# First attention: one product for the maxima ahead of the value products in each unit and one behind them

## The chip, the cores and the metric

The kernel runs on one core of one Trainium2 chip. The time is the device time of one execution in microseconds (us), and the figure compared is the median of several runs. The engines work side by side and meet at semaphores: TensorE (PE, its weight loads shown apart as PEld), VectorE (DVE), ScalarE (ACT), GpSimd (POOL) and the DMA queues, here above all SyncE's (SP).

## The reference

The whole is two layers over 8 images of 384 tokens and 256 channels: edges of an image joined with text, a first attention, an FP4 feed-forward, an anchor attention and a mixture of experts. The change touches the first attention alone:

```python
q, k, v, kp = (_heads(x @ W.T) for W in (W_Q, W_K, W_V, W_K_prime))   # 16 heads of 16
attn   = softmax(q k^T / 4)
attn_p = softmax(q kp^T / 4)
out = alpha * (attn v) + (1 - alpha) * (attn_p v)
return out @ W_O.T
```

16 heads times the two kinds of keys (k and kp) are 32 softmaxes over 384x384 scores for each image.

## The kernel before

`attention0` (from L122) writes out the instruction stream of each engine. `for_images` (L286) calls a function `turn` for images 0 to 7: images 1 to 4 in a hardware loop of two images a pass, the others straight. Text and trace are told here by these names.

**A unit** is one softmax: `turn` (L568 on PE) runs 32 units v for image i, in groups of four (g = v // 4, j = v % 4). In a unit PE issues, in this order:

- S: the transposed scores (`scores`, matmul at L516), two products into banks 4 and 5, then after one R a third into bank 6. ACT turns them into `prob` by exponentials (L706).
- R: products for the maxima (`ring`, L503). The softmax of the next image needs the maximum of each row of its scores, so the scores of image i+1 are computed a first time in the other orientation, 128x384 a product, and DVE reduces each to one maximum a row (`tensor_reduce`, L819). There are 96 such entries for an image, and two entries (48 and 97) that are a transpose of the maxima found (T, L500), from which DVE makes the negated maxima `mneg` (L823, L826) for SP to spread (L322). The entries use banks 0 to 2 in turn: entry r waits until the reduction of entry r-3 has ended (`ring_free`), and a T until all earlier ones have. The first entry of an image waits for all of the image before.
- V: the value products (`values`, L527), four heads side by side in 32 columns each, eight records in bank 7. They belong to the group before: V of units j = 1, 2, 3 is one third each. Units with j = 0 have none, nor have units 1 to 3 of image 0.
- a step in bank 3, where `BANK3` names one for the unit: projections of a later image (L473, L481), transposes (L464, L536, L542) or the output product (L550). It waits until the other engines have emptied bank 3 from the step before.

`ring_part(v)` gives a unit three entries, here called R1, R2 and R3; units 15 and 31 have a fourth, T. DVE's `turn` (L907) reduces the unit's entries and then does its part of the step: `low_parts` (L808), `normalize` (L841, L845), `add` (L854) with the moments behind it (L861). At the start of an image it first does `inputs` (L797). Image 7 has no entries to make, since no image follows.

The order in a unit is thus S S R1 S V R2 R3 (T) step, and S S R1 S R2 R3 step where there is no V.

Of the kernel before, what the change touches and what calls it, by code (L numbers as in the profile page):

```python
# [121 lines left out]
def attention0(nc, G, x, txt, scharr, wq, wk, wv, wkp, wo, alpha, wgate, wup, wdown, fp4_dram):  # L122
# [18 lines left out]
    def ring_part(v):  # L141

        return range(NR * v // UNITS, NR * (v + 1) // UNITS)
# [19 lines left out]
    def edge_piece(r):  # L163

        j, n = divmod(r - len(PREPARE), len(TAPS))
        return (j + BESIDE, n) if 0 <= j < B - BESIDE else (None, None)
# [6 lines left out]
    def bank3(v, prev, more, more2):  # L173

        step, n = BANK3.get(v, (None, 0))
        of = {"turn_outputs": -1 if n >= GROUPS - 2 else 0, "values": 1, "turn_y": -1, "output": -1,
              "inputs": 2, "project": 2, None: None}[step]
        if step is None or not {-1: prev, 0: True, 1: more, 2: more2}[of]:
            return None, 0, 0
        return step, n, of  # L180

    with ExitStack() as ctx:
# [113 lines left out]
        with nc.Block() as block:  # L296
# [163 lines left out]
            def _(pe):  # L460
# [24 lines left out]
                def ring(i, b, entries):  # L485

                    for r in entries:
                        u, t = RING[r]
                        if r in (0, NR // 2):
                            for m in range(3):  # L490
                                signal = stack_in[r // (NR // 2)][m]
                                pe.wait_ge(signal.sem, signal.at(i, 16 * len(SLOTS)))

                        back = 3 if t is not None else 1
                        if r >= back:
                            pe.wait_ge(ring_free.sem, ring_free.at(i, r - back + 1))
                        elif not isinstance(i, int) or i:
                            pe.wait_ge(ring_free.sem, ring_free.at(i, 0))
                        if t is None:
                            mm = pe.transpose(ps[0:2 * NM, r % 3, 0:P], mx[:, u:u + 2].rearrange("p n k h t -> p (n k h t)"),  # L500
                                              ident[:])
                        else:
                            mm = pe.matmul(ps[:, r % 3, 0:T], qs[0:NS, b, u // 2, t * P:(t + 1) * P],  # L503
                                           ks[0:NS, b, u % 2, u // 2], start=True, stop=True)
                        mm.then_inc(ring_full.sem, 1)

                def scores(i, b, v, part):

                    hh, kp = v // (2 * QUAD) * QUAD + v % QUAD, v // QUAD % 2
                    if v % HALF == 0 and part == 0:  # L510
                        signal = mrow_in[v // HALF]
                        pe.wait_ge(signal.sem, signal.at(i, signal.per))

                    pe.wait_ge(exp_done.sem, exp_done.at(i, max(2 * v + part - 1, 0)))
                    for t in PARTS[part]:
                        mm = pe.matmul(ps[:, 4 + t, 0:T], ks[0:NS + 4, b, kp, hh, t * P:(t + 1) * P],  # L516
                                       qs[0:NS + 4, b, hh], start=True, stop=True)
                    mm.then_inc(st_done.sem, 1)

                def values(i, b, g, t):  # L520

                    if t == 0:
                        pe.wait_ge(exp_done.sem, exp_done.at(i, 2 * QUAD * (g + 1)))

                        pe.wait_ge(o_done.sem, o_done.at(i, g))
                    for j in range(QUAD):
                        mm = pe.matmul(ps[j * SLOT:(j + 1) * SLOT, 7, 0:T],  # L527
                                       vp[:, b, t, g // 2 * QUAD + j], prob[:, g % 2, j, t],
                                       start=(t == 0), stop=(t == TT - 1), tile_position=(0, j * SLOT))
                    if t == TT - 1:  # L530
                        mm.then_inc(av_done.sem, 1)
# [27 lines left out]
                def in_bank3(step, i, n, last):  # L559

                    if last:
                        signal, image, count = last
                        pe.wait_ge(signal.sem, signal.at(image, count))
                    do, signal = STEPS[step]
                    do(i, n)
                    return signal, i, n + 1

                def turn(i, b, prev, more, more2):  # L568

                    last = (y_done, i - 1, GROUPS - 2) if prev else (rest_done, 1, 3 * KC)  # L570
                    for v in range(UNITS):
                        g, j = v // QUAD, v % QUAD
                        scores(i, b, v, 0)
                        if more:
                            ring(i + 1, 1 - b, ring_part(v)[:1])
                        scores(i, b, v, 1)
                        if j and g:
                            values(i, b, g - 1, j - 1)
                        elif j and prev:
                            values(i - 1, 1 - b, GROUPS - 1, j - 1)  # L580
                        if more:
                            ring(i + 1, 1 - b, ring_part(v)[1:])
                        step, n, of = bank3(v, prev, more, more2)
                        if step:
                            last = in_bank3(step, i + of, n, last)
# [55 lines left out]
                for r in range(FIRST):  # L641
# [3 lines left out]
                    i, n = edge_piece(r)  # L645
# [4 lines left out]
                pe.wait_ge(vp_ready.sem, 1)  # L650
                pe.wait_ge(mag_done.sem, mag_done.at(B - 1, 2))
                for_images(pe, turn)

                i = B - 1
# [1611 lines left out]
```

## Time and profile before

| | us |
|---|---|
| median of three runs | 1908.77 (1907.85 to 1909.83) |
| profiled execution, its own time | 1910.5 |
| span of the profile, first to last instruction | 1908.7 |
| of it, first attention's units with entries (images 0 to 6) | 140 to 666 |
| PE busy | 1774.1 (93%) |
| DVE busy | 1025.9 (54%) |
| ACT busy | 679.3 (36%) |
| DVE reductions for the maxima, L819, 768 of them | 383.6 |
| PE products R, L503, 768 of them | 221.6 |
| mean granted clock of PE | 0.974 of 2.4 GHz |

A row of the timeline has the start, the time from there to the end of the last of its instructions, the engine, the line, output and input, the count, and in brackets how long the engine had been idle and who released it. A single product's duration includes the way through the array, so products that follow each other closely start nearer together than they take. "x2" is two instructions merged into one row.

### The profile page before, as it was taken

Reading aid. Unit: us, or ns where it says so; the run is one execution under the profiler, and the core shown is the slowest. Engines: PE = TensorE matmul, PEld = TensorE weight load, DVE = VectorE, ACT = ScalarE, POOL = GpSimd, SP = SyncE. Lnnn points to the kernel's source line nnn. Section 1 sums busy time; section 2 is a strip of 40 time slices with the busy share of each in tenths; the row PEclk is TensorE's granted clock in tenths of the full one; section 3 lists DMA queues with packets and bytes.
Section 4 is the critical chain, followed back from the end, with each engine's and each line's share of the span. In section 5 each row is a group of like instructions: output and inputs, shape, how many; then the busy total and the mean of one; then the engine's idle time right before and its main releaser. Section 6 shows DMA issues by size and latency. Waiting matters only on the chain. (4 is left out here: it accounts for less than half of the span.)

```text
span 1908.7 us, 29136 instructions
## 1 busy us (share of the span) xinstructions
PE 1774.1 (93%) x9935; PEld 1121.4 (59%) x9935; DVE 1025.9 (54%) x2071; ACT 679.3 (36%) x1292; POOL 398.9 (21%) x415
## 2 busy tenths in 40 slices
PE   7989999899999994888899999997999999999997
PEld 3324444444444333566665656565666668999997
DVE  6587877777778874788876445542321121222221
ACT  2115656556556673444444223322211110111110
POOL 2101021020210001677662211220032121010010
PEclk9979999999999996999999999998999999999999
DMA  5833643635436023000009000000010012242211
GB/s 186 137 51 64 88 76 39 103 62 65 76 61 91 2 71 126 19 0 0 0 6 375 3 0 0 0 1 1 0 42 33 17 36 97 101 167 99 100 36 32
DMA packets 112675, 117.56 MB, mean 62 GB/s; under 512 B 11535, under 2 KB 104513, under 8 KB 112322
## 3 DMA queue, kind: packets, MB, share of 16 engines
q1 hardware_dynamic: 99330, 87.93, 21.8%
q10 hardware_dynamic: 9600, 18.92, 2.8%
q0 software_dynamic: 3648, 9.46, 1.3%
q8 instruction: 55, 0.90, 0.2%
q14 instruction: 42, 0.34, 0.1%
HBM read 80.87 MB, written 35.29 MB: 61 GB/s over the span
## 5 line engine op out<-in xcount | busy, mean ns | idle before, releaser
L819 DVE TENSOR_REDUCE mx<-ps_a 128x1 f32<-128x384 f32 x768 | 383.6, 551 | 70.0 <-PE ps_a L503 67.8
L706 ACT ACTIVATE prob<-ps_a 128x768 f32<-128x768 f32 (+1 forms) x512 | 306.2, 650 | 119.8 <-PE ps_a L516 119.7
L503 PE MATMUL ps_a<-ks,qs 96*128 96x384 bf16 x768 | 221.6, 340 | 12.0 <-DVE mx L819 4.7
L516 PE MATMUL ps_a<-qs,ks 100*128 100x384 bf16 x768 | 210.3, 334 | 6.5 <-issue 3.8
L2029 PEld LDWEIGHTS ps_e<-xTr,w 128*128 128x128 f32 x1792 | 204.4, 192 | 2.2 <-issue 0.8
L2029 PE MATMUL ps_e<-xTr,w 128*128 128x128 f32 x1792 | 204.7, 275 | 0.6 <-DVE xTr L2202 0.6
L1965 PE MATMUL ps_e<-xT_all,w 128*128 (+1 forms) x512 | 170.4, 492 | 0.9 <-ACT xT_all L2056 0.9
L503 PEld LDWEIGHTS ps_a<-ks,qs 96*128 96x128 bf16 x768 | 61.9, 98 | 181.0 <-DVE mx L819 119.9
L527 PE MATMUL ps_a<-prob,vp 128*32 128x384 f32 x1536 | 164.7, 502 | 0.0
L1514 PE MATMUL ps_m<-w 128*128 128x352 f32 x384 | 125.0, 470 | 21.7 <-ACT w L1677 21.3
L1965 PEld LDWEIGHTS ps_e<-xT_all,w 128*128 128x128 f32 x512 | 97.7, 192 | 66.5 <-issue 1.8
L2092 ACT ACTIVATE gel_r<-ps_e 128x512 f32<-128x512 f32 x56 | 33.5, 597 | 280.5 <-PE ps_e L2029 280.5
L516 PEld LDWEIGHTS ps_a<-qs,ks 100*128 100x128 bf16 x768 | 72.0, 99 | 75.8 <-ACT prob L706 27.2
L2109 DVE TENSOR_TENSOR hid_e<-gel,ps_e 128x384 f32<-128x384 f32 x64 | 35.5, 554 | 137.1 <-ACT gel L2062 137.1
L1514 PEld LDWEIGHTS ps_m<-w 128*128 128x128 f32 x384 | 70.3, 192 | 61.8 <-issue 23.9
L2062 ACT ACTIVATE gel<-ps_e 128x384 f32<-128x384 f32 x64 | 31.5, 492 | 207.9 <-PE ps_e L1965 207.9
L2038 PE MATMUL ps_e<-w,hid_r 128*128 128x256 f32 x448 | 101.3, 379 | 0.0
L1476 POOL TENSOR_TENSOR attn<-lg,gsum 128x1024 f32<-128x1024 f32 x24 | 45.6, 1901 | 234.9 <-DVE gsum L1378 234.9
L2213 DVE TENSOR_TENSOR hid_r<-gel_r,ps_e 128x512 f32<-128x512 f32 x56 | 38.5, 688 | 100.6 <-ACT gel_r L2092 100.6
L1581 PE MATMUL ps_m<-wsT,xT_a 128*128 128x512 f32 x192 | 87.1, 596 | 4.8 <-DVE lg L1369 4.8
L442 POOL TENSOR_TENSOR y<-y 128x192 f32<-128x192 f32 x32 | 19.9, 621 | 332.5 <-DVE y L845 332.5
L2038 PEld LDWEIGHTS ps_e<-w,hid_r 128*128 128x128 f32 x448 | 82.9, 190 | 10.1
(242 smaller groups left out, 2519.7 us busy)
## 6 DMA issues: line engine op xcount, KB each, us to landing
ks<-parts_dram SPq DMA_DIRECT2D x192, 96.0 KB, 6.3
w<-in_L_ffn_W_dram ACTq DMA_DIRECT2D x18, 1024.0 KB, 8.2
parts_dram<-parts SPq DMA_DIRECT2D x24, 576.0 KB, 3.9
qs<-parts_dram SPq DMA_DIRECT2D x96, 96.0 KB, 4.2
prob<-in_x_dram SPq DMA_DIRECT2D x24, 256.0 KB, 3.6
w<-in_L_ffn_W_dram SPq DMA_DIRECT2D x6, 1024.0 KB, 13.0
grouped_x<-empty_row SPq DMA_DIRECT2D x1, 4352.0 KB, 24.6
grouped_h<-empty_row SPq DMA_DIRECT2D x1, 4240.5 KB, 33.1
```

The lines of the kernel that those rows point to most:

```text
L503: mm = pe.matmul(ps[:, r % 3, 0:T], qs[0:NS, b, u // 2, t * P:(t + 1) * P], ks[0:NS, b, u % 2, u // 2], start=True, stop=True)
L516: mm = pe.matmul(ps[:, 4 + t, 0:T], ks[0:NS + 4, b, kp, hh, t * P:(t + 1) * P], qs[0:NS + 4, b, hh], start=True, stop=True)
L527: mm = pe.matmul(ps[j * SLOT:(j + 1) * SLOT, 7, 0:T], vp[:, b, t, g // 2 * QUAD + j], prob[:, g % 2, j, t], start=(t == 0), stop=(t == TT ...
L706: act.activation(prob[:, g % 2, j, ts.start:ts.stop], ps[:, 4 + ts.start:4 + ts.stop, 0:T], ACT.Exp).then_inc(exp_done.sem, 1)
L819: dve.tensor_reduce(at, ps[:, r % 3, 0:T], AX.X, ALU.max).then_inc(ring_free.sem, 1)
L1476: pool.tensor_tensor(attn[:, b, t].rearrange("p (h a) -> p h a", a=A1), lg[:, t % 2].rearrange("p (h a) -> p h a", a=A1), gsum[:, t % 2, 1 ...
L1514: mm = pe.matmul(ps[:, 2 * (u % 2) + n, 0:HALF0], xT[:, t, k], wguT[:, n, k, s * HALF0:(s + 1) * HALF0], start=(k == 0), stop=(k == KC - 1))
L1581: mm = pe.matmul(ps[:, bank + n], xT1[:, k, t * P:(t + 1) * P], wsT[:, k, n * 512:(n + 1) * 512], start=(k == 0), stop=(k == KC - 1))
L1965: mm = pe.matmul(ps[:, 2 * (a % 2) + m, 0:T], w12[:, 0, m, k, a * P:(a + 1) * P], xT_all[:, i, k], start=(k == 0), stop=(k == KC - 1))
L2029: mm = pe.matmul(ps[:, 2 * n + m, a * P:(a + 1) * P], w12[:, b, m, k, n * HALF1 + a * P:n * HALF1 + (a + 1) * P], xTr[:, k], start=(k == 0 ...
L2038: mm = pe.matmul(ps[:, 4, 0:C], hid_r[:, a], w3[:, b, a], start=(a == 0), stop=(a == IT1 - 1))
L2213: dve.tensor_tensor(hid_r[:, n * 4:(n + 1) * 4].rearrange("p a t -> p (a t)"), gel_r[:, n], ps[:, 2 * n + 1], ALU.mult).then_inc(rhid_done ...
```

## The change

In a unit, the second of its entries (R2) is issued ahead of V, straight behind the third score product, and the rest (R3, and T where there is one) stays behind V. Before, both stood behind V. The entries keep their numbers, banks and order among each other, and the number of instructions is the same. DVE, ACT, POOL and SP keep their order.

```diff
                         scores(i, b, v, 1)
+                        if more:
+                            ring(i + 1, 1 - b, ring_part(v)[1:2])
                         if j and g:
                             values(i, b, g - 1, j - 1)
                         elif j and prev:
                             values(i - 1, 1 - b, GROUPS - 1, j - 1)
                         if more:
-                            ring(i + 1, 1 - b, ring_part(v)[1:])
+                            ring(i + 1, 1 - b, ring_part(v)[2:])
```

Where a unit has no V the two calls follow each other and the order is the one before. With V it becomes S S R1 S R2 V R3 (T) step.

## Rows read from the trace of the kernel before

**Rows 1.** Stages view, image 1's stretch: busy time and count by engine, clock, DMA.

```profile
225.00:310.00 85.00, 80.95 (x533) 37.35 (x532) 65.44 (x144) 52.62 (x97) 11.43 (x17) 1.00 0.50 74
```

**Rows 2.** Waits of PE from 140 to 667: total, times, longest.

```profile
PE ps_a L500 <- DVE mx L819: 14.2, 15, 1.0
```

**Rows 3.** Instructions of tile ps_a: durations in ns (least, median, most), starts, forms.

```profile
L527 PE MATMUL ps_a<-prob,vp x1536: 486/498/849, 153.3 to 721.4; 128*32 128x384 f32 x192
...
L819 DVE TENSOR_REDUCE mx<-ps_a x768: 524/549/560, 76.7 to 665.7; 128x1 f32<-128x384 f32 x192
```

**Rows 4.** Timeline of unit 30 of image 1, without a step.

```profile
285.69 0.49 PE L516 MATMUL ps_a<-qs,ks 100*128 100x384 bf16 x2
...
286.18 0.33 PE L516 MATMUL ps_a<-qs,ks 100*128 100x384 bf16 x1
...
286.44 0.85 PE L527 MATMUL ps_a<-prob,vp 128*32 128x384 f32 x8
287.22 0.11 PEld L503 LDWEIGHTS ps_a<-ks,qs 96*128 96x128 bf16 x2 [0.62 <-DVE mx L819]
287.22 0.50 PE L503 MATMUL ps_a<-ks,qs 96*128 96x384 bf16 x2
...
287.56 0.49 PE L516 MATMUL ps_a<-qs,ks 100*128 100x384 bf16 x2
287.60 1.49 DVE L819 TENSOR_REDUCE mx<-ps_a 128x1 f32<-128x384 f32 x3 [0.38 <-PE ps_a L503]
```

**Rows 5.** Timeline: R2 and R3 of units without V, first, one in full, last.

```profile
159.73 0.80 PE L503 MATMUL ps_a<-ks,qs 96*128 96x384 bf16 x2
...
282.24 2.42 DVE L819 TENSOR_REDUCE mx<-ps_a 128x1 f32<-128x384 f32 x5 [0.38 <-PE ps_a L503]
...
282.86 0.79 PE L503 MATMUL ps_a<-ks,qs 96*128 96x384 bf16 x2
...
283.49 0.49 PE L536 MATMUL ps_a<-ident,osb 128*128 128x128 f32 x3
...
658.59 0.79 PE L503 MATMUL ps_a<-ks,qs 96*128 96x384 bf16 x2
```

**Rows 6.** Timeline: last reductions ahead of T in unit 31 of image 1.

```profile
289.47 1.02 DVE L819 TENSOR_REDUCE mx<-ps_a 128x1 f32<-128x384 f32 x2 [0.38 <-PE ps_a L503]
...
290.55 0.31 PE L500 MATMUL ps_a<-ident,mx 128*96 128x128 f32 x1 [0.95 <-DVE mx L819]
```

**Rows 7.** Timeline: the same in unit 15, behind a low_parts.

```profile
251.66 0.55 DVE L819 TENSOR_REDUCE mx<-ps_a 128x1 f32<-128x384 f32 x1
...
252.37 1.02 DVE L819 TENSOR_REDUCE mx<-ps_a 128x1 f32<-128x384 f32 x2 [0.16 <-PE ps_a L503]
...
253.45 0.31 PE L500 MATMUL ps_a<-ident,mx 128*96 128x128 f32 x1 [0.95 <-DVE mx L819]
```

**Rows 8.** Timeline of units 22 to 24 of image 1, behind the moments.

```profile
272.82 1.93 DVE L819 TENSOR_REDUCE mx<-ps_a 128x1 f32<-128x384 f32 x4
...
273.42 0.34 PE L503 MATMUL ps_a<-ks,qs 96*128 96x384 bf16 x1
...
275.63 0.80 PE L503 MATMUL ps_a<-ks,qs 96*128 96x384 bf16 x2
```

**Rows 9.** Timeline of units 0 to 2 of image 2, behind `inputs`.

```profile
292.98 1.48 DVE L819 TENSOR_REDUCE mx<-ps_a 128x1 f32<-128x384 f32 x3
...
293.59 0.34 PE L503 MATMUL ps_a<-ks,qs 96*128 96x384 bf16 x1 [0.49 <-DVE mx L819]
...
295.58 0.34 PE L503 MATMUL ps_a<-ks,qs 96*128 96x384 bf16 x1
```

**Rows 10.** Timeline of PE, image 7: first f32 products straight behind V.

```profile
697.28 0.92 PE L550 MATMUL ps_a<-wT,yT 128*128 128x256 f32 x3
```

**Rows 11.** Stages view: first units of images 1 and 2, columns as in Rows 1.

```profile
213.00:219.00 6.00, 5.29 (x25) 2.37 (x26) 4.43 (x12) 2.50 (x4) 0.00 (x0) 0.72 0.05 10
290.00:296.00 6.00, 4.58 (x28) 1.94 (x28) 5.01 (x15) 2.92 (x5) 0.00 (x0) 1.00 0.04 11
```

## The prediction

> **What bounds the kernel now.** I read the stages first, then the waits of PE, then the timeline of one image unit by unit. In the stretch of image 1 PE is busy 80.95 of 85 us at full clock, DVE 65.44, ACT 52.62 [rows 1]: PE sets the pace, and DVE, which only has to give three banks back in time, is the engine that makes it wait. The change moves work on PE from one place to another and takes nothing away. It can gain only what PE stands still for DVE, so those standstills have to be found and priced one by one. The waits view names one kind, the transpose T behind the last reductions: 14.2 us in 15 places [rows 2]. It hides the rest, because a product's recorded duration covers short holes; these have to be read from the distance of starts.
>
> A clean unit with V and without a step takes 287.56 - 285.69 = 1.87 us [rows 4]. Where products follow each other, starts are 0.165 us apart (two take 0.49 to 0.50, one 0.33). From the third S to V is 286.44 - 286.18 = 0.26, so 0.09 goes on the turn to the four narrow tiles. From V to R2 is 0.78, and R2 to the next S is 0.34, two products [rows 4]. DVE starts 0.38 after R2 does (287.60 against 287.22), and a chain of reductions takes 0.55 for the first and about 0.47 for each more (three in 1.49) [rows 4], although one alone takes 0.549 [rows 3]. From the end of a reduction to the product that waited for it is about 0.06.
>
> **The change part by part.** Unit with nothing late: S to R2 0.165, R2 to V 0.26, V to R3 0.78, R3 to the next S 0.165. That is the same 1.87. R2 has the shape of the S ahead of it, so I take 0.26 for the turn to the tiles as it stands, and the number of turns doesn't change. Effect 0, for 165 units (21 of image 0, 24 in each of images 1 to 6). The V records themselves are untouched (498 ns median) [rows 3]. V ends 0.165 later, and with it ACT's copy of bank 7; ACT has slack for that in the units where the copy stands, and the turn of its result comes a unit later.
>
> (a) Units without V. In these R3 comes only 0.99 us after the R3 of the unit before, and must wait for that one's reduction. In unit 28 of image 1 the two R records take 0.79 where 0.49 is the clean value: 0.30 us of standstill [rows 5]. The reason is that R2 and R3 of unit 27 come out together behind V, at 281.86 and 282.03. DVE starts at 282.24, needs 0.55 + 0.47 for the two, and is through at 283.26; R3 of unit 28 starts at 283.32. After the change R2 of unit 27 has been reduced while V ran, and R3 alone is behind V, at the same 282.03: reduction from 282.41 to 282.96, product free at 283.02, where its clean place is. I take 0.28 of gain (bounds 0.2 and 0.30, the whole standstill). Such records of 0.79 or 0.80 stand, the first at 159.73 and the last at 658.59 [rows 5], in units 8, 20, 24, 28 of image 0, units 24 and 28 of images 1 to 5, and units 12, 24, 28 of image 6: 17. Unit 24 of images 1 to 6 is special, next paragraph, so 11 x 0.28 = 3.1 us.
>
> (b) Unit 24 of images 1 to 6. Here DVE is behind by the moments. Its reductions of unit 22 start at 272.82 and end at 273.37, 273.83 and 274.30; R1 of unit 23 is held by the first until 273.42 [rows 8]. R2 of unit 23, moved ahead, would like to start 0.33 later at 273.75, but waits for the second, until 273.90: a new wait of 0.15, and V, R3 and all the rest stand behind it on PE. In return R3 of unit 24 (275.63, 0.80 for two [rows 8]) no longer waits. Net 0.30 - 0.15 = 0.15, six times: 0.9 us.
>
> (c) The transposes T. R2, R3 and T now: DVE starts at 289.47, takes 1.02 for two, T starts at 290.55, 1.46 after R2 [rows 6]. Changed: R3 starts 0.165 later than R2 did, its reduction 0.38 on, 0.55 long, T 0.06 on: 1.16. Gain 0.29. It holds for units 31 of images 0 to 6 and unit 15 of image 6, 8 places. In unit 15 of images 0 to 5 DVE begins R1's reduction late, at 251.66, behind a `low_parts` [rows 7]. Then R1 ends at 252.21, R2 at 252.68, R3 at 253.15, and T comes at 253.21 against 253.45 now: 0.24. Sum 8 x 0.29 + 6 x 0.24 = 3.8 us. What follows T (the negated maxima, `inputs`, the next image's R1) hangs on T and moves with it. Bounds: 0.2 and 0.47 (one reduction less with nothing given back) a place, so 2.8 to 6.6.
>
> To this last one the Trainium skill has a rule, in "VectorE: DVE Perf Modes", section "The DRAIN you can't avoid": a next operation doesn't start before the pipe of the one before has emptied. By it the pair would cost 2 x 0.549 and (c) would give some 0.08 more at each T, in all about 1 us. The rows of pairs say 1.02, so the trace disagrees, and I stay with the rows.
>
> (d) Places where the new R2 has to wait ahead of V. Rule: R2 of a unit waits for the second reduction of the unit before. It bites where DVE is late. In units 0 to 2 of image 2 the reductions of unit 0 start at 292.98 behind `inputs`, and R1 of unit 1 already waits for the first, until 293.59 [rows 9]. The second ends at 294.00, so R2 goes at 294.07 where it would like 293.92: 0.15. In unit 2 R1 waits until 295.58 now [rows 9], 0.11 late; changed, that wait is hidden in the delay, but R2 waits again, 0.12. Net loss 0.15 for images 2 and 4, where unit 1 has this standstill: 0.3 us. Images 1, 3 and 5 start at half clock and have no such wait, image 6 has no `inputs`. Behind `normalize` (units 26 and 30) I find R2 about 0.1 free. If that is misjudged it costs up to 0.1 in 14 units, 1.4 us. Behind `low_parts` the second reduction of the unit before is done long before.
>
> **The sum.** 3.1 + 0.9 + 3.8 - 0.3 = 7.5 us. All of it is on PE's path: PE runs the stage, the next stage starts behind a barrier, and image 7 is unchanged. SP's transfers for later images hang on DVE's and POOL's steps, which keep their places. The profiled execution took 1910.5 of its own, 1.8 over its span and 1.7 over the median; it would come to 1903.0, and the median of 1908.8 to 1901.3. With the bounds of (a), (c) and (d) the gain is 4.6 (2.2 + 0.9 + 2.8, less 0.3 and about 1) to 10.5 (3.3 + 0.9 + 6.6, less 0.3).
>
> **The rivals.**
>
> Half the gain. The places of (a) don't open, because the third bank is short again: R3's reduction ends 0.02 or less ahead of where R3 wants to go, so any delay of DVE by a tenth brings it back. Against it: in unit 28 DVE has been idle 0.38 before the R3 reduction [rows 5]. Only (c) is left, with 0.3 off: 3.5, the time 1905.3.
>
> Nothing. The standstills move from R3 and T to R2, as far as DVE is the real limit of those stretches, or something else is next late (ACT's exponentials, the emptying of bank 3). For it: around T several engines wait. Against it: DVE is idle before the reductions in question [rows 5, 6], so it isn't the limit. 1908.8.
>
> Slower: the load of weights isn't hidden behind a single product. Now two products of one shape stand between V and the rest, and their two loads are done together, 0.11 for both [rows 4]. Behind the change the load for a step's f32 product, or for S, has only one product of 0.165 to hide under. That loads can stick out behind V is seen where f32 products follow it directly: the first three take 0.92 [rows 10], 0.11 more than three starts 0.215 apart and a last duration of 0.38. If each of the 165 units paid about 0.10, that would be 16.5 us, less 7.5: 9.0 slower, 1917.8. It decides from 7.5 / 165 = 0.045 us a unit on. Against it: the second load starts at once in today's order, and R3's stream of 0.165 is longer than the 0.11. The Trainium skill speaks for this rival, in "TensorE: Matmul & The Clock Gate", section "Part 3: Packing small matmuls — row/col tiling": a load overlaps running matmuls only where the row groups differ, and these products use the same rows. The trace disagrees for plain products, whose loads start with the product before them.
>
> More: the clock. At half clock the first units of image 1 cost more than those of image 2: PE is busy 5.29 of 6 us for 25 products at a granted clock of 0.72, against 4.58 for 28 at 1.00 [rows 11]. The clock fell there behind T and the longer stop at the edge of the loop. Each of four such edges could be spared or moved by shorter stops: up to 0.8 us each, 2 us or so in all, 1899.3.
>
> **How the numbers follow.** Forecast 1901.3, chance 0.62. More by the clock 0.10, half 0.13, nothing 0.07, slower 0.08. A measurement of this kernel can tell about 0.2% from no change, 3.8 us; the line is at 1905.0. Half the gain falls on either side of it: 0.07 faster, 0.06 the same. Faster 0.79, same 0.13, slower 0.08. The forecast's own bounds give 1898.3 to 1904.2. With the half case taken in at one end and the clock at the other, 1898.8 to 1905.2 leaves out the cases of no gain and of slower (0.15) and a thin tail at the fast end, together under 0.2.
>
> **What would show it.** In unit 30, S to R2 0.165, R2 to V 0.26, V to R3 0.78 and 1.87 in all: if the unit is longer, the slower rival is at work. The two R of unit 28 back to 0.49. T's wait behind R3 about 0.99 after R3's start instead of 1.28. R2 of unit 23 and of unit 1 waiting about 0.15 ahead of V. The stretch from image 1's to image 2's T about 1 us shorter, and the first attention's last R 7.5 us earlier. DVE's busy time and its 768 reductions should stay. The prediction is wrong if ACT or the emptying of bank 3 shows up as the new releaser in these places, or if a wait ahead of V turns up in the units with steps.

## The result and the profile after

The changed kernel takes 1896.5 us, the median of 9 runs (1894.5 to 1898.8). The kernel before has a median of 1906.8 over nine runs, three of which are those that the prediction started from; one of the others took 6035.7 and is left out of the ratio. The ratio is 0.995, with a 95% interval of 0.9936 to 0.9964. That is a gain of 9.5 us (6.9 to 12.2) by the ratio, 10.3 between the medians, and 12.3 on the base of 1908.8 that the prediction was made against. The prediction said 1901.3 (1898.8 to 1905.2) and a gain of 7.5. The sign was right, and the time fell below the range.

The profiled execution took 1897.8, with a span of 1896.0, 12.7 less than before. Of the 12.7, 8.9 lie between the first S of image 0 and that of image 7 (517.4 against 526.3), where the change is; 0.1 lies ahead of it and 3.7 behind, in stages that the change doesn't touch. The head of the page of the changed kernel (busy time, share of the span, instructions):

```profile
PE 1768.3 (93%) x9935; PEld 1120.0 (59%) x9935; DVE 1022.3 (54%) x2071; ACT 682.5 (36%) x1292; POOL 398.9 (21%) x415
PEclk8989999999999997999999999998999999999999
```

The granted clock by slices on the page of the kernel before:

```profile
PEclk9979999999999996999999999998999999999999
```

The counts are the same and DVE's work is nearly so (1025.9 before); the time went out of holes on PE. The clock rows differ in three of the 40 slices: the first and the third (9 and 7 before, 8 and 8 here), both ahead of the units, and the sixteenth (6 before, 7 here), behind them. A slice is 47 us long, and a short stretch at half clock at the edge of an image doesn't show in it.

The stages view of the changed kernel, one stretch in image 1 (it answers to [rows 1]) and its edge (to [rows 11]). The image begins 1.9 us earlier here, and the windows are 5 and 3 us earlier, so they don't cut it at quite the same place:

```profile
220.00:305.00 85.00, 81.76 (x536) 38.51 (x536) 64.37 (x144) 52.53 (x96) 11.43 (x17) 1.00 0.52 79
210.00:216.00 6.00, 4.47 (x32) 1.64 (x24) 4.53 (x13) 3.49 (x7) 0.00 (x0) 1.00 0.02 3
```

PE gets 536 products into 85 us instead of 533, all at full clock. From the first S of image 1 to that of image 2 it is 75.46 instead of 76.96. From image 1's T to image 2's it is 75.57 instead of 76.25, both without an edge at half clock: 0.7 less, where the prediction had said about 1. At the edge of image 1, where before had a clock of 0.72, this execution has 1.00.

The waits of PE between 139 and 658 us, changed kernel (total, times, longest), against [rows 2]:

```profile
PE ps_a L500 <- DVE mx L821: 10.2, 15, 0.9
PE ps_a L503 <- DVE mx L821: 1.8, 4, 0.6
```

T waits 4.0 us less in its 15 places, of which 14 are in the units that changed (the first stands ahead of image 0). The predicted gain of 3.8 there is met.

**The places one by one**, from the timelines. First unit 28 of image 1, where R2 and R3 took 0.79 before [rows 5], and the start of unit 29 (rows: start, time to the end of the last, engine, line, output and input, count, in brackets idle time and releaser):

```profile
279.17 0.34 PE L503 MATMUL ps_a<-ks,qs 96*128 96x384 bf16 x1
279.35 0.49 PE L516 MATMUL ps_a<-qs,ks 100*128 100x384 bf16 x2
279.55 1.51 DVE L821 TENSOR_REDUCE mx<-ps_a 128x1 f32<-128x384 f32 x3 [0.36 <-PE ps_a L503]
279.87 1.19 ACT L708 ACTIVATE prob<-ps_a 128x768 f32<-128x768 f32 x2
280.00 0.49 PE L503 MATMUL ps_a<-ks,qs 96*128 96x384 bf16 x2
280.33 0.49 PE L536 MATMUL ps_a<-ident,osb 128*128 128x128 f32 x3
...
280.74 0.34 PE L516 MATMUL ps_a<-qs,ks 100*128 100x384 bf16 x1
```

The pair R2, R3 is back to 0.49, as forecast. But the unit, S to S, is 1.39 (280.74 - 279.35), and not the 1.32 that its products would need (six starts of 0.165 and three transposes in 0.33). The next S is now held by ACT, as the distances show: the exponentials start 0.52 after S, two take 1.19 together, the first about 0.81 of it, and the next S starts 0.06 after that, at 1.39. The trace of the kernel before has this length already where no R was late, as in unit 20 of image 5 (578.15 - 576.75, with the two R in 0.49):

```profile
576.75 0.49 PE L516 MATMUL ps_a<-qs,ks 100*128 100x384 bf16 x2
577.28 1.19 ACT L706 ACTIVATE prob<-ps_a 128x768 f32<-128x768 f32 x2 [1.98 <-PE ps_a L516]
577.41 0.49 PE L503 MATMUL ps_a<-ks,qs 96*128 96x384 bf16 x2
...
578.15 0.50 PE L516 MATMUL ps_a<-qs,ks 100*128 100x384 bf16 x2
```

Unit 31 of image 1, then T of unit 15:

```profile
284.98 0.33 PE L516 MATMUL ps_a<-qs,ks 100*128 100x384 bf16 x1
285.15 0.33 PE L503 MATMUL ps_a<-ks,qs 96*128 96x384 bf16 x1
285.40 0.85 PE L527 MATMUL ps_a<-prob,vp 128*32 128x384 f32 x8
286.19 0.34 PE L503 MATMUL ps_a<-ks,qs 96*128 96x384 bf16 x1
286.56 0.56 DVE L821 TENSOR_REDUCE mx<-ps_a 128x1 f32<-128x384 f32 x1 [0.36 <-PE ps_a L503]
287.18 0.31 PE L500 MATMUL ps_a<-ident,mx 128*96 128x128 f32 x1 [0.65 <-DVE mx L821]
```

```profile
250.66 0.31 PE L500 MATMUL ps_a<-ident,mx 128*96 128x128 f32 x1 [0.69 <-DVE mx L821]
```

The pattern of a unit is the predicted one: S to R2 0.17, R2 to V 0.25, V to R3 0.79, R3 to T 0.99. In front of T stands one reduction of 0.56, where [rows 6] had two in 1.02.

Unit 1 of image 2, with the new wait ahead of V. R1 is held as before [rows 9], and R2 comes 0.47 behind it, where 0.33 would be clean:

```profile
290.22 0.34 PE L503 MATMUL ps_a<-ks,qs 96*128 96x384 bf16 x1 [0.49 <-DVE mx L821]
...
290.69 0.34 PE L503 MATMUL ps_a<-ks,qs 96*128 96x384 bf16 x1
290.95 0.85 PE L527 MATMUL ps_a<-prob,vp 128*32 128x384 f32 x8
```

### The profile page after: what moved, and what is told of

Read it like the earlier page. It is cut to its first block and busy times, and to the rows that moved or that the text cites. A ratio compares the mean times of both kernels' runs of the same rounds, so it can differ in the third digit from the quotient of the medians.

```text
span 1896.0 us, 29136 instructions
## 1 busy us (share of the span) xinstructions
PE 1768.3 (93%) x9935; PEld 1120.0 (59%) x9935; DVE 1022.3 (54%) x2071; ACT 682.5 (36%) x1292; POOL 398.9 (21%) x415
## 5 line engine op out<-in xcount | busy, mean ns | idle before, releaser
L503 PE MATMUL ps_a<-ks,qs 96*128 96x384 bf16 x768 | 244.1, 338 | 10.0 <-DVE mx L821 5.5
L503 PEld LDWEIGHTS ps_a<-ks,qs 96*128 96x128 bf16 x768 | 74.5, 98 | 188.7 <-DVE mx L821 103.2
```

## The experiments

Each kernel's time was taken in five rounds against the kernel before on the same chip. Chips and rounds differ by more than some of the effects, so a ratio is always to the kernel before beside it. "Unit" lengths are the distance from S to the next S, in stretches at full clock, as differences from the kernel before. The diffs are in PE's `turn`, against the kernel before unless told otherwise.

**c_before and c_after**: the two kernels again, unchanged, as the measure for the rest.

> The kernel before, unchanged, measured again beside the others, for its spread and its granted clock. The profile of the changed kernel shows the forecast holes closing (about 6.6 us by their own sizes), yet the profiled span fell by 12.7. Theory A: the rest is the clock; the kernel before loses full clock at the edges of image 1, 3, 5 and 7, where PE stands still longest, and in most executions it shows a lower mean clock than the changed kernel: ratio 1.000, mean clock about 0.974, the changed one 0.979. Rival B: the difference of clocks is chance of the executions first shown; then both kernels have the same mean clock over ten executions, this one's median lies at about 1904, and the changed one is 6 to 7 us below it.

> The changed kernel, unchanged, on the same chip. Theory A (holes 6.6 us plus a higher clock): ratio about 0.995, mean granted clock higher by 0.003 to 0.005 than the kernel before in most executions. Rival B (chance of the clock): ratio about 0.9965, equal clocks.

Measured: the kernel before 1904.7 (12 runs, 1901.1 to 1907.5), after 1895.6 (6 runs), ratio 0.9955 (0.9941 to 0.997). The kernel before has a median of 1904.8 over 29 runs of this chip, 1906.1 over 23 on a second, 1904.5 over 12 on a third; single runs go from 1899.8 to 1912.0. The three runs that the prediction started from, with 1908.8, lie near the upper end of this. The mean clock is 0.9766 and 0.9793. So neither expectation holds whole: the kernel before isn't as slow as A had it, and the changed kernel's clock isn't the same, as B had it.

Comparing these two, unit by unit, gives what each place of the change is worth:

```
unit                                  measured   forecast
8, 20, 24, 28 of image 0; 12, 28 ...   -0.227     -0.28     (a), 11 places
23 of images 1 to 6                    +0.137     +0.15     (b)
24 of images 1 to 6                    -0.227     -0.30     (b)
31 of images 0 to 6, S to T            -0.30      -0.29     (c)
15 of images 0 to 5                    -0.257     -0.24     (c)
15 of image 6                          -0.30      -0.29     (c)
1 of images 1, 2 and 4                 +0.138     +0.15, images 2 and 4 only (d)
18 of image 6                          +0.083      0
the unit behind one that got shorter   +0.012      0
other units with V                     +0.003      0
```

Images 3 and 5 can't be compared at unit 1 in this pair, since the kernel before ran there at half clock. For image 5 the profile of e_fill, with the old order at full clock, has 2.26 and the changed kernel 2.40: +0.14 there too. Image 3 runs at half clock there in all twelve profiles.

**e_t_only**: R2 goes ahead in units 15 and 31 alone. **e_rest_only**: in all units but these.

```diff
+                        ahead = 2 if v in (15, 31) else 1      # e_t_only
+                        ahead = 1 if v in (15, 31) else 2      # e_rest_only
+                        if more:
+                            ring(i + 1, 1 - b, ring_part(v)[1:ahead])
...
-                            ring(i + 1, 1 - b, ring_part(v)[1:])
+                            ring(i + 1, 1 - b, ring_part(v)[ahead:])
```

> R2 goes ahead of V in units 15 and 31 alone, the other units keep the order of before. Forecast's part (c): 8 x 0.29 + 6 x 0.24 = 3.8 us, T 0.99 us after R3 (1.03 in unit 15 behind low_parts) instead of 1.28, and R3 of units 24 and 28 still held (the two R records 0.79). If the clock gain of theory A comes from shorter stops at T, this kernel has it too: gain 6 to 8 us and a mean clock like the changed kernel's. If the clock has to do with something else, the gain is 3.8.

> R2 goes ahead of V in all units but 15 and 31. Forecast's parts (a), (b) and (d): holes 3.1 + 0.9 - 0.3, by the sizes seen in the changed kernel's profile 3.2 + 1.0 - 0.6 - about 0.8 for units that became 0.005 us longer: 2.8 us. T 1.28 us after R3 as before. If shorter stops at T bring the clock gain, this kernel hasn't got it: gain about 3 us, mean clock like before. If the clock is chance, it lies anywhere between the two.

Measured: e_t_only 1900.8, ratio 0.9981 (0.9971 to 0.9992); e_rest_only 1903.8, ratio 0.9995 (0.9982 to 1.0009). In e_t_only the pair of unit 28 keeps its 0.80, and T waits 0.65 instead of 0.95:

```profile
276.16 0.80 PE L503 MATMUL ps_a<-ks,qs 96*128 96x384 bf16 x2
...
283.56 0.31 PE L500 MATMUL ps_a<-ident,mx 128*96 128x128 f32 x1 [0.65 <-DVE mx L822]
```

In e_rest_only it is the other way round:

```profile
284.78 0.50 PE L503 MATMUL ps_a<-ks,qs 96*128 96x384 bf16 x2
...
286.24 0.31 PE L500 MATMUL ps_a<-ident,mx 128*96 128x128 f32 x1 [0.95 <-DVE mx L822]
```

So the terms stand apart as the prediction had them, and no place pays for another: from unit 16 to 31 an image gains 0.28 by the one and 0.30 by the other, and 0.57 by both. The gain at the T's is larger than all the rest of the change together. The times are less additive than the units: against the runs of c_before, spans fall by 4.2 and 0.7 on average, and by 8.7 with both. The interval of e_rest_only includes no change, so its forecast gain of 2.8 stands in its units alone. What is missing goes with the clock, below. e_t_only also answers its own question: it has the shorter stops at every T and a mean clock of 0.9772, and not the 0.979 of the changed kernel.

**e_both_ahead**: R2 and R3 both ahead of V, so that nothing but V stands in front of the step.

```diff
+                        ahead = 3
```

> R2 and R3 both ahead of V in every unit. Against the changed kernel, by holes: T of unit 31 and of image 6's unit 15 comes about 0.46 us earlier (8 times, 3.7), unit 15 of images 0 to 5 is held by DVE behind low_parts and gains nothing, R3 gets its own wait ahead of V in units 1 and 2 of images 1 to 5 and in unit 23 of images 1 to 6 (about 0.3 each more, 2.5 and 1.8). Sum about 0.6 slower than the changed kernel: ratio 0.996. If clean units get longer by it, the turn to the tiles costs more than taken.

Measured: 1911.4, ratio 1.0021 (1.0011 to 1.0032), slower than the kernel before, although unit 31 is 0.745 shorter. The expectation, 0.6 slower than the changed kernel, was wrong: the units take 12.4 more than in c_after. The T's give 3.4, and the waits ahead of V in units 1, 2 and 23 cost 3.8, much as expected (unit 1 is now +0.43 and unit 23 +0.437 against before). What it lacked is 11.2 us. R3 also waits ahead of V in units 13, 17 and 21 and, behind `normalize`, in 26 and 30 (6.5 together, the dearer step of the first three included). And a step that stands directly behind V costs more in the others (4.7): units with projections or the output product +0.09, with transposes +0.04, although nobody is late there. The timeline of e_both_ahead at a projection:

```profile
256.65 0.62 PE L503 MATMUL ps_a<-ks,qs 96*128 96x384 bf16 x2
256.93 0.10 PEld L503 LDWEIGHTS ps_a<-ks,qs 96*128 96x128 bf16 x1 [0.34 <-DVE mx L822]
257.20 0.85 PE L527 MATMUL ps_a<-prob,vp 128*32 128x384 f32 x8
257.98 1.56 PE L473 MATMUL ps_a<-xT,wT 128*128 128x384 f32 x4
```

The four f32 products take 1.56; with one R product between V and them they take 1.46 (the next kernel's first row). The weight loads of these four products begin only at 257.98, together with the first of them, and the second product starts 0.43 behind the first, where the later ones start 0.32 apart. In the changed kernel the first of these loads begins under R3. This is the mechanism of the slower rival, at about the 0.11 that it read from [rows 10]. It needs V directly in front. One product of 0.165 in between hides the load fully: in the changed kernel nearly all units with steps are unchanged within 0.005.

**e_best**: what the places teach, put together. In unit 31 (and 15 of image 6) R2 and R3 go ahead of V, since there T has nothing else to wait for; in unit 15 of images 0 to 5 T goes behind the projection, which fills its wait; units 1 and 2 keep the old order; all others have the order of the change.

```diff
+                        late_t = v == 15 and more2
+                        ahead = 1 if v in (1, 2) else 3 if v == 31 or v == 15 and not more2 else 2
...
-                            ring(i + 1, 1 - b, ring_part(v)[1:])
+                            ring(i + 1, 1 - b, ring_part(v)[ahead:3 if late_t else None])
                         step, n, of = bank3(v, prev, more, more2)
                         if step:
                             last = in_bank3(step, i + of, n, last)
+                        if more and late_t:
+                            ring(i + 1, 1 - b, ring_part(v)[3:])
```

> The changed kernel, but: in unit 31 (and unit 15 of image 6) R2 and R3 both ahead of V; in unit 15 of images 0 to 5 T goes behind the unit's projection, which then fills the wait; units 1 and 2 keep the order of before. By holes, against the changed kernel: 8 x 0.46 = 3.7, 6 x about 0.5 = 3.2 (the wait of 0.8 filled, 0.1 given back at R3 of unit 16 and 0.2 at its low_parts), 0.14 in image 1 to 5 = 0.6. Together 7.5 us: about 1888, ratio 0.991 to 0.992. If the clock follows the stops, a little less time still. If the chain from T to the negated maxima is what sets the pace behind it, part of the 7.5 comes back as a wait of the next image's R1.

Measured: 1890.0 (1887.1 to 1892.4), ratio 0.9914 (0.9897 to 0.993), the fastest of all kernels here. Unit 31 is 0.75 shorter than before, unit 15 is 1.19 shorter (3.27), unit 16 is 0.38 longer, as the transposes there now wait for `rest`; unit 1 is back. Over the images the units take 7.2 us less than in c_after, near the 7.5 expected. Its timeline around T of unit 15 and of unit 31:

```profile
245.51 1.46 PE L473 MATMUL ps_a<-xT,wT 128*128 128x384 f32 x4
246.80 0.27 PE L500 MATMUL ps_a<-ident,mx 128*96 128x128 f32 x1
...
248.71 0.54 PE L536 MATMUL ps_a<-ident,osb 128*128 128x128 f32 x3 [0.54 <-DVE rest L814]
...
281.89 0.31 PE L500 MATMUL ps_a<-ident,mx 128*96 128x128 f32 x1 [0.30 <-DVE mx L825]
```

T waits for nothing in unit 15 and 0.30 in unit 31, where the changed kernel has 0.69 and 0.65.

**e_fill and e_after_fill**: the question of the clock. In unit 31 the stop ahead of T is filled with products that nobody reads (five in the kernel before, four in the changed kernel), and T's time isn't meant to move.

```diff
-                            ring(i + 1, 1 - b, ring_part(v)[1:])
+                            ring(i + 1, 1 - b, ring_part(v)[1:3])    # [2:] and [2:3] in e_after_fill
+                            if v == UNITS - 1:
+                                signal, image, count = last
+                                pe.wait_ge(signal.sem, signal.at(image, count))
+                                for _ in range(5):           # 4 in e_after_fill
+                                    pe.matmul(ps[:, 3, 0:T], qs[0:NS, 1 - b, H0 - 1, 0:P],
+                                              ks[0:NS, 1 - b, 1, H0 - 1], start=True, stop=True)
+                            ring(i + 1, 1 - b, ring_part(v)[3:])
```

> The kernel before, with five more products of R's shape into bank 3 (whose content nobody reads any more) in the standstill ahead of T of unit 31 of images 0 to 6. They run 5 x 0.165 = 0.83 us inside a wait of about 1.28, so T comes when it came and the holes theory alone says: no change, ratio 1.000. They leave PE standing 0.45 us there instead of 1.28. Theory A (shorter stops at an image's edge keep the clock up): mean granted clock over the executions rises from 0.9765 towards 0.979 and the time falls by 2 to 4 us. Rival B (the clock has to do with something else, the stops' length doesn't matter): clock 0.9765, ratio 1.000.

> The changed kernel with four such products ahead of T of unit 31 (0.66 us inside a wait of about 0.99). Theory A: clock 0.979 or a little more, time as the changed kernel or 1 us below it, ratio 0.9955 to 0.995. Rival B: the same time as the changed kernel.

The timeline of e_fill shows that T stays where it was, 1.45 behind R2, with PE at work until then:

```profile
287.97 0.50 PE L503 MATMUL ps_a<-ks,qs 96*128 96x384 bf16 x2
288.31 0.98 PE L587 MATMUL ps_a<-ks,qs 96*128 96x384 bf16 x5
289.42 0.31 PE L500 MATMUL ps_a<-ident,mx 128*96 128x128 f32 x1
```

Measured: e_fill 1904.7, ratio 0.9993 (0.9982 to 1.0005), mean clock over its runs 0.9771 against 0.9757 of the kernel before beside it; e_after_fill 1897.6, ratio 0.9951 (0.9935 to 0.9967), clock 0.9792. In the kernel before the clock rises a little, in the changed kernel (0.979 in its first runs) it doesn't. That fits shorter stops as a part of the reason, but the interval of e_fill includes no change, and its clock goes half of the way at most: a hint, not shown.

**e_long**: the changed kernel with an extra reduction, whose result nobody reads, ahead of the last one before T in unit 31, so that T is late again while everything else has the new order. **c_after2**: the changed kernel, unchanged, beside it.

```diff
+        spare = sb("spare", [P, 1])
...
+                            if r == NR - 2:
+                                dve.tensor_reduce(spare[:], ps[:, r % 3, 0:T], AX.X, ALU.max)
                             dve.tensor_reduce(at, ps[:, r % 3, 0:T], AX.X, ALU.max).then_inc(ring_free.sem, 1)
```

> The changed kernel with one reduction more on DVE, made a first time into a spare tile and not used, ahead of the last reduction of unit 31 of images 0 to 6. PE's stop at T there grows by about 0.5 us, to 1.5 behind R3 in place of 0.99, longer than in the kernel before; everything else stays. By holes alone: 7 x 0.5 = 3.5 us more than the changed kernel, clock as the changed kernel's (0.979). Theory A (the length of the stops at an image's edge decides how often the clock falls): mean clock down to about 0.9765 and 5 to 7 us more. Rival B: 3.5 and the clock stays at 0.979.

> The changed kernel once more, for its mean clock and as the neighbour of the next one. As before it: ratio 0.995 to 0.9955, mean granted clock about 0.979 against 0.9757 to 0.9765 of the kernel before.

Measured: c_after2 1898.7, ratio 0.9969 (0.9958 to 0.9981), a gain of 5.8 at nearly equal clocks (0.9776 against 0.9769); the 0.979 and the ratio of 0.995 that were expected didn't come again. e_long 1917.0, ratio 1.0069. Its unit 31 is 0.47 longer than that of the changed kernel, as forecast:

```profile
284.72 0.56 DVE L823 TENSOR_REDUCE spare<-ps_a 128x1 f32<-128x384 f32 x1 [0.36 <-PE ps_a L504]
285.20 0.55 DVE L824 TENSOR_REDUCE mx<-ps_a 128x1 f32<-128x384 f32 x1
285.80 0.32 PE L501 MATMUL ps_a<-ident,mx 128*96 128x128 f32 x1 [1.12 <-DVE mx L824]
```

From the T ahead of image 0's first unit to the last T it lost 4.1 us, 3.3 of them ahead of T in seven units 31 and 0.8 at edges. In its profile the edges of images 1, 3 and 7 have half clock, in that of c_after2 only image 3's. But its total can't be read, because a stage in which not one instruction differs became 10 us longer. The stages view over that stage, e_long and then c_after2:

```profile
739.20:1323.80 584.60, 531.58 (x2741) 354.16 (x2741) 358.56 (x552) 216.63 (x458) 224.97 (x178) 0.99 0.11 39
```

```profile
734.00:1308.30 574.30, 531.41 (x2741) 354.68 (x2741) 348.06 (x552) 216.42 (x458) 228.03 (x178) 0.99 0.12 40
```

DVE is busy 10.5 us more with the same 552 instructions. The traces say where: 9.2 us are the 48 instructions of one line (L1272 in e_long, L1269 in c_after2), and 1.2 those of another. Over 128x16 such an instruction takes 0.17 to 0.18 where no GpSimd instruction is under way when it starts, and up to 1.68 when POOL has just begun an instruction of 1.68 of its own. The same step in c_after2, where DVE is first by 0.03, and in e_long, where it comes 0.29 behind POOL:

```profile
796.73 0.18 DVE L1269 SCALAR_TENSOR_TENSOR w<-w 128x16 f32<-128x16 f32 x1
796.76 1.68 POOL L1452 TENSOR_TENSOR w<-w 128x704 f32<-128x704 f32 x1 [3.26 <-ACT w L1704]
```

```profile
801.75 1.67 POOL L1455 TENSOR_TENSOR w<-w 128x704 f32<-128x704 f32 x1 [3.27 <-ACT w L1707]
...
802.04 1.42 DVE L1272 SCALAR_TENSOR_TENSOR w<-w 128x16 f32<-128x16 f32 x1
```

In e_long 9 of the 48 take less than 0.32, in the other eleven profiles 19 to 21, and these 48 sum to 43.3 against 33.3 to 34.2. What shifted the two engines against each other in e_long was not found.

## Why the prediction was right or wrong

**The base, and the clock left out of the sum: together they put the time outside the range.** Two steps failed. One is "the median of 1908.8 to 1901.3" under **The sum**, and with it the range, which was made of the bounds of the terms alone. The other is that the clock stood at nothing in the sum, as a rival in place of the forecast and not as a term beside it (below). On the base measured beside it the forecast gain gives 1899.3, and the measured 9.5 on the old base gives 1899.3 too: either alone stays in the range. On the 1904.8 of the later runs the base alone is enough. The median of three runs was taken as exact, though their spread of 2 us was no measure of what other sets of runs give: 64 later runs have medians of 1904.5 to 1906.1. On 1904.8 the forecast gain of 7.5 gives 1897.3, and on the 1906.8 measured beside the changed kernel 1899.3. Of the 4.8 us between 1901.3 and 1896.5, 2.0 are the base of those runs and 2.8 more gain than forecast (10.3 by medians); against the changed kernel's other runs (1895.6 on 1904.7) it is 4.1 and 1.6.

**(c), the transposes: right.** 8 x 0.30 + 6 x 0.257 = 3.9, forecast 3.8. e_t_only alone gave 4.2 us of span against c_before. That chained reductions of one pair take 1.02 and a single one 0.56 was the reading that decided it.

**(a), units without V: right place, too large.** 11 x 0.227 = 2.5, forecast 3.1. The pair R2, R3 did come back to 0.49, but the unit can't be shorter than 1.39, the turn of ACT's exponentials. The prediction named ACT as a possible next in line, gave it no price, and called its appearance in these places a sign of being wrong; it did appear, in the 11 places of (a) and in the six units 24 of (b). The trace of before could have given the price: a unit without V took 1.62 from S to S there, its own products need 1.32, the exponentials' start and duration (0.52 and 0.81) give the floor, and unit 20 of images 5 and 6 took 1.39.

**(b): right in kind.** Unit 23 loses 0.137 (forecast 0.15), unit 24 gains 0.227 (0.30, the same floor): 6 x 0.09 = 0.5, forecast 0.9.

**(d): too small.** Unit 1 loses 0.14 as forecast, but in images 1, 2, 4 and 5 and not in two. Images 1, 3 and 5 were left out because they had started at half clock in the one profile that I had. Image 3 does so in all twelve profiles, and what unit 1 loses there was not measured; images 1 and 5 do so in some alone, so a place may not be left out because one profile shows it slow. About 0.6 and not 0.3. The 0.1 of spare in units 26 and 30 was there.

**Effect 0 in the clean units: nearly.** 0.012 in the 17 units behind one that got shorter, 0.003 in the others with V and 0.083 in unit 18 of image 6 make about 0.6 us in all, a term that the sum didn't have. It is too small to see in one unit and shows only in averages over the images.

So the places give 2.5 + 0.5 + 3.9 - 0.6 - 0.6 = 5.7 us, against the forecast 7.5: the gain of the mechanism itself was forecast too high, and both (a) and the two losses are inside or near the bounds given. c_after2, where the clocks are nearly equal, measured 5.8. That the forecast of 7.5 lies near the measured 9.5 is in part luck: the places were put 1.8 too high, and the clock's part was left out.

**The clock: left out of the sum, and it came on top.** Elsewhere the gain is larger, 9.1 us of mean span on the first chip, and these runs of the changed kernel have a mean clock of 0.9793 against 0.9766. Over 41 runs of the kernel before, the span falls by 15.5 us for 0.01 of clock; over the 15 runs of the changed kernel ahead of c_after2 it falls by 8.9, with c_after2's by 12.6. By these slopes 0.0027 is worth 2.4 to 4.2, and 5.7 with that gives 8.1 to 9.9. Profiles show a part of it. From the T ahead of image 0's first unit to the last T, the two profiles of the kernel before take 526.5 and 525.2, and the three of the changed kernel 517.6, 517.8 and 517.8. The first of before has half-clock edges at images 1, 3, 5 and 7, the second at 3 and 5, all of after only at image 3. So between c_before and c_after 7.4 us lie in the units, 5.7 of them in the places and 1.7 at edges, nearly all at those with half clock. The other 1.4 of the span's 8.9 lie outside, where nothing was changed: 2.9 gained ahead of the units and 1.5 lost behind. The prediction held the clock as an alternative with 0.10 and 2 us; it comes in addition to the other terms, and in two of the three sets of runs of the changed kernel.

That the rest of the gain goes with the clock is what the sets of runs show: 9.1 with 0.9793, and 5.8 with 0.9776. That shorter stops ahead of T spare the edges is borne out by the profiles, one of each kernel: where the stop in unit 31 is as long as before or longer, half clock stands at the edges of images 1, 3, 5 and 7 (before), 3 and 5 (c_before), 1, 3 and 6 (e_rest_only), and 1, 3 and 7 (e_long); in the eight where it is shorter or filled, e_fill among them, only at image 3. That this is the whole of the clock's part is not shown, and three kernels speak against it: e_t_only (0.9772), e_fill (0.9771) and c_after2 (0.9776) have the short or filled stops and stay near the 0.9757 to 0.9769 of the kernel before. Why some sets of runs reach 0.979 stays open.

**Slower by the load of weights: rightly set low.** Rows 10 had the right price. The reason given against it was also right, since the load needs only the one product of 0.165 to hide under; e_both_ahead shows what happens without it. **Half, nothing:** out, since the places of (a) opened. The row given against "half" was misread: the 0.38 of idle time in [rows 5] stands ahead of five reductions that run 2.42 without a pause, not ahead of R3's in unit 28.

**The rule on the DRAIN** ("VectorE: DVE Perf Modes" in the Trainium skill, section "The DRAIN you can't avoid"), as the prediction took it, doesn't fit the changed kernel either: three chained reductions take 1.51 where one takes 0.56. The same section says that "A next op that is not held starts earlier", so the prediction took the rule too strictly, and the rows don't contradict the section as a whole.

## What to carry to other kernels

Price a gap between two waits against every other engine's turn in that unit, and not against the removed wait alone: the shortest turn that is left (here ACT's, 1.39) caps the gain. When a bounded ring of banks feeds a slower consumer, spread its products around the long block so that each finds a free bank, put both in front only where the consumer's last result is what everyone waits for, and keep one short product between narrow-column products and an f32 one. And take the base of a prediction with its own spread: here single runs of one kernel lie 12 us apart, more than the change is worth. An instruction added as a probe can move two engines against each other in a stage far behind it, so read a probe's effect where it was put and not from its total.

## What was not expected of the hardware

- The f32 load directly behind the value products costs 0.09 to 0.10 us (four products 1.56 and not 1.46), and one bf16 product between them takes that to nothing.
- The edge of image 3 starts at half clock in all twelve profiles; those of images 1, 5, 6 and 7 do so in some. The mean clock of the kernel before is 0.9757, 0.9766 and 0.9769 on three chips, and the differences between executions are worth several us in 1905.
- A DVE instruction over 128x16 takes 0.17 us alone and up to 1.68 when a GpSimd instruction of 1.68 has begun just ahead of it; being 0.03 ahead instead saves all of it. In e_long this made an untouched stage 10 us longer (DVE 358.6 us busy instead of 348.1 with 552 instructions).
